# The third chunk of an expert's tokens with 64 rows in place of 128, in a one-core mixture-of-experts kernel

## The reference

```
C = _capacity(T, E)                                   # 320 tokens for each of 8 experts
logits = tokens @ gate_weight.T
top1 = argmax(logits); ranks = cumsum(one_hot(top1)) - 1
mask = mask * (ranks < C)                             # a token past place 320 is dropped
dispatch = einsum('tec,th->ech', sec_mask, tokens)    # the tokens of each expert, by place
hmid = gelu(einsum('ech,ehi->eci', dispatch, wi))     # 512 -> 2048
eout = einsum('eci,eih->ech', hmid, wo)               # 2048 -> 512
out = einsum('tec,ech->th', combine_weights, eout)    # weighted, back to the token's row
```

## Time and profile before

| | us |
|---|---|
| median of 3 runs | 1109.25 |
| lowest, highest of them | 1108.97, 1111.19 |
| the profiled execution | 1110.63 |
| its span, first to last instruction | 1108.9 |
| PE busy | 1049.4 (95% of the span) |
| DVE, ACT, POOL busy | 721.2, 544.1, 142.3 |
| share of PE in the chain that ended last | 91% |
| mean granted TensorE clock | 0.973 of full |

### The profile page before, as it was taken

One profiled execution on the slowest core, in us unless ns is written; L12 is line 12 of the kernel. 1 busy time (PEld: TensorE's weight loads), 2 busy tenths in 40 slices (PEclk: granted clock), 3 DMA queues, 4 the chain that ended last, 5 costly groups with the idle time before them and its releaser, 6 DMA issues.

```text
span 1108.9 us, 20936 instructions
## 1 busy us (share of the span) xinstructions
PE 1049.4 (95%) x7912; PEld 993.3 (90%) x7912; DVE 721.2 (65%) x1089; ACT 544.1 (49%) x851; POOL 142.3 (13%) x135
## 2 busy tenths in 40 slices
PE   7699999999999999599999996999999999999995
PEld 5699989999999999378778775999999999999995
DVE  8456556766676777378786775557767677665652
ACT  5345445655556565154243214455656656554441
POOL 3201101113020210100000012002112021130101
PEclk9699999999999999899999997999999999999998
DMA  8377637475555652400011125446576665654510
GB/s 306 131 269 278 210 115 237 148 249 197 193 198 198 240 178 75 140 37 1 1 38 39 50 105 175 149 152 214 182 238 214 216 226 181 228 206 149 174 38 24
DMA packets 83284, 177.45 MB, mean 160 GB/s; under 512 B 4192, under 2 KB 4704, under 8 KB 83168
## 3 DMA queue, kind: packets, MB, share of 16 engines
q1 hardware_dynamic: 75488, 152.61, 40.2%
q0 software_dynamic: 7168, 23.07, 5.9%
q10 hardware_dynamic: 576, 1.05, 0.3%
HBM read 162.04 MB, written 18.87 MB: 163 GB/s over the span
## 4 chain that ended last, share of the span: by engine, by line
PE 91%; DMA 2%; DVE 2%; ACT 2%; issue 2%; POOL 1%; SPq 0%; POOLq 0%; ACTq 0%; DVEq 0%
PE psH L1212 13%; PE psH L1213 13%; PE psH L1214 13%; PE acc L1219 11%; PE acc L1220 11%; PE acc L1221 11%; PE acc L1212 3%; PE acc L1214 3%; PE acc L1213 3%; PE psT L1431 1%; PE psT L1267 1%; PE acc L1387 1%; PE psH L1387 1%; PE psT L1537 1%; PE psH L1438 1%
## 5 line engine op out<-in xcount | busy, mean ns | idle before, releaser
L1212 PE MATMUL psH<-dth,wih 128*128 128x240 f32 (+5 forms) x1024 | 295.8, 289 | 0.0
L1213 PE MATMUL psH<-dtl,wih 128*128 128x240 f32 (+5 forms) x1024 | 294.1, 287 | 0.0
L1214 PE MATMUL psH<-dth,wil 128*128 128x240 f32 (+5 forms) x1024 | 293.9, 287 | 0.0
L1219 PE MATMUL acc<-hth,woh 128*128 128x240 f32 (+5 forms) x1024 | 293.5, 287 | 0.0
L1220 PE MATMUL acc<-htl,woh 128*128 128x240 f32 (+5 forms) x1024 | 293.3, 286 | 0.0
L1221 PE MATMUL acc<-hth,wol 128*128 128x240 f32 (+5 forms) x1024 | 293.3, 286 | 0.0
L786 DVE TENSOR_TENSOR wol<-raw_wo,woh 128x1024 fp32r<-128x1024 f32 x128 | 155.7, 1223 | 146.6 <-ACT woh L608 146.6
L642 ACT ACTIVATE gel<-psH 128x320 f32<-128x320 f32 x256 | 112.0, 437 | 192.7 <-PE psH L1214 187.5
L608 ACT ACTIVATE woh<-raw_wo 128x1024 fp32r<-128x1024 f32 x128 | 134.2, 1056 | 132.2 <-PE acc L1221 132.1
L1212 PEld LDWEIGHTS psH<-dth,wih 128*128 128x128 f32 x1024 | 193.9, 189 | 0.4
L1213 PEld LDWEIGHTS psH<-dtl,wih 128*128 128x128 f32 x1024 | 193.9, 189 | 0.0
(11 more groups left out here) (194 smaller groups left out, 1152.8 us busy)
## 6 DMA issues: line engine op xcount, KB each, us to landing
raw_wi<-in_wi SPq DMA_DIRECT2D x64, 1024.0 KB, 5.1
raw_wo<-in_wo SPq DMA_DIRECT2D x64, 1024.0 KB, 5.6
out_x<-xt SPq DMA_DIRECT2D x4, 1024.0 KB, 4.9
xt<-in_x SPq DMA_DIRECT2D x6, 512.0 KB, 8.4
xt<-x SPq DMA_DIRECT2D x3, 1024.0 KB, 9.4
raw_u<-in_wuT SPq DMA_DIRECT2D x1, 1024.0 KB, 10.8
raw_u<-in_wvT SPq DMA_DIRECT2D x1, 1024.0 KB, 12.8
xt<-in_x ACTq DMA_DIRECT2D x2, 256.0 KB, 3.7
```

What stands on the lines that cost most here:

```text
L1212: pe.matmul(out, lh, rh, start=first, stop=False)
L1213: pe.matmul(out, lh, rl, start=False, stop=False)
L1214: return pe.matmul(out, ll, rh, start=False, stop=last)
L1219: pe.matmul(out, lh, rh, start=False, stop=False, skip_group_check=True)
```

## The change

```
                 for k in range(CHUNKS):
-                    pool.indirect_dma_start(rows[a][:, k, :], None, source,
-                                            bass.IndirectOffsetOnAxis(ap=src_now[:, a, k:k + 1], axis=0)
+                    m = ROWS[k]
+                    pool.indirect_dma_start(rows[a][0:m, k, :], None, source,
+                                            bass.IndirectOffsetOnAxis(ap=src_now[0:m, a, k:k + 1], axis=0)
                                             ).then_inc(gathered[a][k], 16)
...
-                    act.activation(dn[:, k, :], rows[a][:, k, :], ACT.Identity,
-                                   bias=facts_now[:, a, k, SHIFT:SHIFT + 1],
-                                   scale=facts_now[:, a, k, RSTD:RSTD + 1]).then_inc(s.dn_done, 1)
+                    m = ROWS[k]
+                    act.activation(dn[0:m, k, :], rows[a][0:m, k, :], ACT.Identity,
+                                   bias=facts_now[0:m, a, k, SHIFT:SHIFT + 1],
+                                   scale=facts_now[0:m, a, k, RSTD:RSTD + 1]).then_inc(s.dn_done, 1)
...
                     for k in range(CHUNKS):
-                        q = k * P
-                        ins = pe.transpose(TURNED[c][:, q:q + P], dn[:, k, c * P:(c + 1) * P], ident[:, :])
+                        q, m = k * P, ROWS[k]
+                        ins = pe.transpose(TURNED[c][:, q:q + m], dn[0:m, k, c * P:(c + 1) * P], ident[0:m, 0:m])
                     ins.then_inc(s.tokT_done, 1)
```

## The result

| | before | after |
|---|---|---|
| median of 4 runs on one chip, us | 1109.93 | 1123.15 |
| lowest, highest | 1108.97, 1111.19 | 1119.80, 1124.84 |
| the profiled execution | 1110.63 | 1119.80 |
| its span | 1108.9 | 1118.1 |
| PE busy | 1049.4 | 1062.8 |

The ratio is 1.0115, 95% interval 1.010 to 1.013: 11 to 14 us slower, 13.2 by the medians and 12.7 by the means. The forecast was 1120.4, or 11.1 more than before. Its direction and its rough size of 1% hold. The median lies 0.15 us above the top of the forecast's own range, 1117 to 1123, which was laid around a before of 1109.25 where the four runs here give 1109.93. The profiled execution is the quickest of the four, only 9.2 above that of before; why is told near the end of the account of the prediction.

What follows compares the result with a forecast made beforehand. PE, 91% of the chain of waits, was taken as the bound. Thirteen heads at 0.80 gave 10.4, first experts with gather +0.2 and +0.5: +11.1 us, 1120.4 on the median; own range 1117 to 1123, extended to 1107.5 for the first rival.

Steps and rivals of the forecast that it cites:

- The bound: Whole kernel: PE is 91% of the chain of waits; at 13 expert heads it waits 0.23 us for DVE's dtl.
- the transposes' price: Expert heads: each third transpose costs +0.237 us, 0.091+0.055 into and again out of the narrow tile, less 0.055 for streaming.
- the exposed weights of 0.055: At each tile change the next transpose's weights are not loaded ahead, adding 0.055 us.
- The slack of 0.14: Ordinary heads: PE has 0.14 us in hand before L1393, so 0.95 lost on PE puts 0.80 on the path.
- The head with the instruction stall: One head where PE waits 3.0 us for an instruction: 0.95 disappears behind it, costing nothing, at most 0.8.
- The activation: Third chunk's activation on 64 partitions: costed the same as on 128, gaining nothing.
- The gather: First experts: half the bytes start them 0.8 us earlier in layer 0, 0.19 in layer 1, worth 0.4 and 0.1.
- The first experts: Heads at 1.2 GHz: four third transposes cost 1.16 us, worth 0.58; net of the gather +0.2 and +0.5.
- No cost for the narrow tile: Rival: third transposes take 0.055 us less, 13 heads gain 0, total -0.9, 1108.3; chance 0.24.
- Without exposed weights: Rival: drain costs but weights load beside it, +0.127 a third transpose, 4.8 over 13 heads, about 1114; chance 0.06.
- The full price: Rival: +0.55 us a third transpose at the heads, 27 over 13 heads, about 1137; chance 0.02.
- the transposes set the pace: Rival: heads each gain 0.055 us, layer 1's low clock ends sooner, total -2.5, 1106.7; chance 0.06.

Runs made afterwards that it cites:

- paired: Changed kernel with blocks 1 and 3 turning their third chunk first, so narrow transposes of two blocks adjoin, four tile changes a head, PE waits merged: ratio to before 1.0033.
- grouped: Changed kernel with all four narrow transposes side by side behind the first two full ones, two tile changes a head, PE waits merged: 1115.93 us, ratio to before 1.0049.
- twice: Changed kernel with each narrow transpose done twice in a row into the same place, still eight tile changes a head: ratio to before 1.0133.
- eighty: Changed kernel with 80 rows in place of 64 in the third chunk's gathers, activations and transposes: 1110.03 us, ratio to before 0.9997.
- two_tiny: Kernel before with the third-chunk transposes of blocks 2 and 3 each replaced by a matmul of 2 columns: 1109.99 us against 1109.74.
- turn_only: Kernel before with only the third chunk's transposes cut to 64 rows, gathers and activations left at 128: 1123.78 us, ratio to before 1.0123.
- warm_after: Changed kernel with sixteen added identity matmuls behind each layer's routing, results unused: 1142.82 us, ratio to before 1.0291.
- fetch_only: Kernel before with only the third chunk's gathers and activations cut to 64 partitions, transposes left full: 1109.59 us over 12 runs, ratio to before 0.9994.
- warm_before: Kernel before with sixteen added identity matmuls behind each layer's routing, results unused: 1132.89 us, ratio to before 1.0201.
- warm_eighty: Changed kernel with 80 rows in place of 64, plus sixteen added identity matmuls behind each layer's routing: 1133.71 us, ratio to before 1.0209.
- two_less: Kernel before with the third-chunk transposes of blocks 2 and 3 left out, so four PE instructions fewer: ratio to before 1.0026.

## Why the prediction came out as it did

**The bound, and the transposes' price.** Right. The forecast for a block was 0.327 + 0.237 = 0.564, measured 0.573; twelve in "about 2.2", measured 2.23; starts around the narrow one 0.2 and 0.2 apart, as written. The 0.091 read off strips of 32 columns held for a tile of 64 rows, and so did the exposed weights of 0.055. The Trainium skill's TensorEngine Tiling (Array Packing), Tiling Modes (Key Properties), has the drain at a change of mode; paired, grouped and twice agree, since the cost goes with the number of changes. The Trainium skill's TensorE: Matmul & The Clock Gate, LDWEIGHTS (a weight load goes by columns), agrees too: 0.13 us with 64 rows against 0.14 with 128.

L1438 spoke against a cost, and the forecast set it aside as the weaker evidence. That evidence still stands: in all runs the 128 by 64 transposes follow matmuls of another tile with no gap. So not every change of tile costs, and why the one in the columns to 64 doesn't, where 32 columns and 64 rows do, stays open.

**The slack of 0.14.** Right, and the clearest part. The clear moved by 0.82 where PE had lost 0.92, the first product behind it by 0.78 (unrounded), and an ordinary expert by 46.72 - 45.93 = 0.79, forecast 0.80. Eighty and two_tiny show the other side: 0.14 saved on PE is given back to the wait for dtl. Thirteen heads make 13 x 0.79 = 10.3, forecast 10.4.

**The head with the instruction stall.** Forecast nothing, at most 0.8. In this pair its clear stands at 4.77 behind the first transpose, 5.08 before. But the stall scatters: 4.77, 5.36, 5.59 and 5.05 in after, turn_only, twice and warm_after, 4.54 to 5.08 (mean 4.88) in the six kernels with the order of before (before, fetch_only, eighty, two_tiny, warm_before, warm_eighty). So nothing, or a few tenths.

**Activation and gather.** The activation cost nothing less, 0.81 on 64 partitions as on 128. The gather was overrated. These are the rows of the changed kernel ahead of the first expert of layer 0 and layer 1, which answer to the earlier trace rows:

```profile
37.94 0.92 POOL L476 DMA_INDIRECT rows<-in_x,src_now  x1 [0.30 <-issue]
...
41.41 1.52 ACT L627 ACTIVATE dn<-rows,facts_now 128x512 f32<-128x512 f32 x2 [1.63 <-DMA rows<-in_x,src_now]
...
43.07 1.89 PE L1389 MATMUL acc<-ident,dn 128*128 128x128 f32 x6 [8.39 <-ACT dn L627]
...
681.99 0.92 POOL L476 DMA_INDIRECT rows<-out_x,src_now  x1 [0.30 <-issue]
...
686.86 1.38 PE L1389 MATMUL acc<-ident,dn 128*128 128x128 f32 x4 [9.64 <-ACT dn L627]
```

From the third gather's issue to the first transpose it is 5.13 us in layer 0 (5.54 before) and 4.87 in layer 1 (4.66 before): 0.4 sooner and 0.2 later, where 0.8 and 0.19 sooner were forecast. Each is one execution, and fetch_only finds nothing in 12 runs. The other profiles say much the same. From the third gather's issue to its activation in layer 0 it is 3.35 to 4.19, mean 3.80, in the five with 64 rows (after, fetch_only, paired, grouped, twice), and 4.15 to 4.58, mean 4.28, in the four with 128 (before, turn_only, two_less, two_tiny). In layer 1 the means are 4.20 and 4.17. There, in all five, the third activation starts right behind the second, 0.72 later, so the wait is for the second gather, which has its 128 rows as before; the forecast looked at the third gather alone.

**The first experts.** This is the term of the sum that was wrong. Its step was that a third transpose costs 0.29 there, four 1.16, "worth 0.58 if the clock rises when it did". The first part holds: the twelve take 3.65 against 2.61, 1.04 more. The condition does not hold: the clock does not rise when it did. The stretches at half clock around the first experts of the changed kernel, which answer to the first and third of the earlier trace rows:

```profile
36.40:50.00 13.60, 6.93 (x31) 4.98 (x32) 4.37 (x10) 5.97 (x9) 4.68 (x5) 0.50 0.53 178
678.10:695.10 17.00, 8.24 (x35) 6.30 (x36) 6.73 (x21) 5.97 (x9) 5.74 (x6) 0.50 0.43 142
```

From the first transpose to the rise it is now 50.0 - 43.1 = 6.9 and 695.1 - 686.9 = 8.3 us; before it was 4.1 and 5.7. In the six such heads of after, turn_only and twice it is 6.6 to 8.3, mean 7.5; in the fourteen of the seven kernels with at most four changes (before, fetch_only, eighty, two_less, two_tiny, paired, grouped) 3.8 to 6.0, mean 5.0. The two groups don't overlap. The 2.5 us more of half clock are worth half, 1.25 a layer. For the profiled pair the sum closes: 1.04 / 2 + (6.94 - 4.12) / 2 = 1.93 in layer 0 and 0.52 + (8.27 - 5.74) / 2 = 1.79 in layer 1, measured 1.88 and 1.74. With the clock up beforehand the excess is gone (0.62 and 0.72, about what an ordinary head pays). That eight changes go with a later rise is shown. The reason is not. It may be the gaps between the transposes, or that the dense products start later: 6.25 to 6.7 us behind the first transpose in the six heads, 4.4 to 5.3 in the fourteen. No run has the one without the other.

**The sum again, with what was measured.** Thirteen heads 10.3, first experts 1.9 + 1.7 = 3.6, gather -0.4 and +0.2: +13.7, against +13.2 by the medians and 12.7 by the means. The forecast had +0.2 and +0.5 for the first experts and the gather together; against +3.4 here, and that is the whole of the missing 2 us and a little more. That the sum agrees this closely is partly luck: its terms for the first experts and the gather come from one execution of each kernel, and the third experts are left out of it.

**The profiled execution of the changed kernel** lies lower, at +9.2. It starts its first transpose 1.74 sooner (43.07 against 44.81), 0.4 of it by the gather and the rest in the routing. And it lacks the stretch at half clock behind the third expert's head: this is the same place as the second line of the earlier trace rows, at full clock here.

```profile
158.00:164.00 6.00, 4.55 (x37) 3.82 (x37) 3.53 (x7) 2.40 (x5) 0.00 (x0) 1.00 0.04 11
```

That expert lasts 53.48 against 55.33, 1.85 less. The stretch is there in the profiles of turn_only and twice and absent in those of after and warm_after, so it is not tied to the change alone. The nine profiles with at most four changes all have it. Whether eight changes make it rarer, four profiles can't tell; if they do, some executions get back up to 1.7 us of what the change costs. Whoever took the difference of the two profiles for the effect would read 9 us, not 13.

**The rivals.** No cost for the narrow tile is refuted by every run with it. Without exposed weights a block would be 0.454, it is 0.573. The full price would be 0.88. That the transposes set the pace in the kernel before is refuted by eighty, two_less and two_tiny: less work there, the same clear.

No version beats both kernels. Eighty rows (1110.03) takes the smaller operands without the price and gains nothing, since PE has slack to give only where it already waits.

## What to carry to other kernels

If such narrow pieces can't be avoided, put them side by side, or stop at more than 64 rows (80 was tried). Before pricing a saving on the engine that bounds the kernel, look at what that engine waits for at that place: here 0.14 us of slack swallowed each gain and only a seventh of the loss. And where work is added while the clock is at half, ask also whether the clock then rises later: here the 2.5 us of delay cost 1.25 us a layer, more than the added work itself (0.52).

## What the runs showed of the hardware

- A change between a 128 by 128 and a 64 by 128 tile delays the next fp32 transpose by 0.09 us at full clock, and its weights (0.055 more than the matmul before hides) come on top, at the change and once behind it. The 0.09 is the same as for strips of 32 columns. Transposes with 128 rows and 64 weight columns behind full ones show no such delay.
- A 64-row transpose more beside another one adds 0.06 us (0.245 for four, twice against after); 80 rows and 80 columns stream faster than 128 with no gap (0.75 for six with two such, against 0.82).
- The clock rose from 1.2 to 2.4 GHz later when the head after the idle time had eight changes of tile: 6.9 and 8.3 us from the first transpose, 4.1 and 5.7 before.
- With four PE instructions fewer in the program two more expert heads waited for an instruction, some 4.5 us at the two heads; with tiny matmuls in the place of the four they did not.
- Matmuls that wait for nothing started 6.5 and 8.9 us behind the last ones of the routing, where only three branches to code used later stand between: idle time ahead of a wait for data need not be that wait.
